# A two-layer perceiver in one launch: transposed inputs, regrouped first cross attention, and the second cross attention's normalisation and shift placed elsewhere

## What is computed

```python
x = x + _L0_xattn_ref(_layernorm(x), ctx, ctx, mask, Wq, bq, Wk, bk, Wv, bv, Wo, bo)  # 16 heads of 8
x = x + _L0_attn_ref(_layernorm(x), ...)      # delta rule over the tokens
x = x + _L0_ffn_ref(_layernorm(x), ...)       # 8 experts, the best 2
x = x + _L1_xattn_ref(ctx, _layernorm(x), Wq, Wkv, Wout, gm, bm, gl, bl)  # 8 heads of 64
x = x + _L1_attn_ref(_layernorm(x), ...)      # gated delta rule
x = x + _L1_ffn_ref(_layernorm(x), ...)       # attention, then 8 experts, the best 2
```

## Time and profile before

| | us |
|---|---|
| time, median of 3 (lowest, highest) | 3080.18 (3079.72, 3081.09) |
| profiled execution, its own time | 3079.37 |
| its span, first to last instruction | 3077.6 |
| mean granted TensorE clock | 0.962 |
| busy in the span: PE / DVE / ACT / POOL | 2819.4 / 1978.6 / 1479.6 / 1906.0 |

### The profile page before, as it was taken

How to read it: one execution, slowest core, us unless ns; L and a number is a source line. 1 busy time by engine, 2 the same in 40 slices (tenths; PEclk the granted TensorE clock), 3 DMA queues, 4 the chain that set the end, 5 groups by cost and what they waited for, 6 DMA issues and landing times. The chain is left out here.

```text
span 3077.6 us, 66754 instructions
## 1 busy us (share of the span) xinstructions
PE 2819.4 (92%) x22718; PEld 1618.6 (53%) x22765; DVE 1978.6 (64%) x4504; ACT 1479.6 (48%) x2385; POOL 1906.0 (62%) x1278
## 2 busy tenths in 40 slices
PE   5799999999999978998899999999999997888789
PEld 2355555555555566775344444444444443777356
DVE  5477777777777744114667767767767744776653
ACT  3466666666666522333544444444444434223633
POOL 5487878787878721001488888888888872553500
PEclk8899999999999989998999999999999998999789
DMA  7655555555555210001000000000000000000300
GB/s 184 187 174 193 177 190 181 184 186 179 194 175 188 100 58 1 1 0 39 22 33 21 21 32 21 21 32 21 21 32 21 21 1 9 3 3 2 85 5 10
DMA packets 146463, 233.18 MB, mean 76 GB/s; under 512 B 16787, under 2 KB 85851, under 8 KB 146076
## 3 DMA queue, kind: packets, MB, share of 16 engines
q1 hardware_dynamic: 145180, 228.87, 22.7%
q10 hardware_dynamic: 1152, 2.49, 0.6%
HBM read 147.80 MB, written 83.52 MB: 75 GB/s over the span
## 5 line engine op out<-in xcount | busy, mean ns | idle before, releaser
L444 POOL TENSOR_TENSOR sb_a_acc<-sb_a_acc,sb_a_PT 128x1024 f32<-128x1024 f32 x252 | 596.7, 2368 | 36.6 <-ACT sb_a_PT L522 30.3
L522 ACT ACTIVATE sb_a_PT<-ps_a_SC 128x1024 f32<-128x1024 f32 (+1 forms) x416 | 425.8, 1023 | 315.3 <-PE ps_a_SC L794 291.7
L607 DVE TENSOR_REDUCE sb_a_mx<-ps_a_A 128x1 f32<-128x512 f32 x768 | 506.4, 685 | 97.0 <-PE ps_a_A L771 91.8
L1686 POOL TENSOR_TENSOR sb_a_acc<-sb_a_acc,sb_a_PT 128x512 f32<-128x512 f32 (+2 forms) x384 | 487.5, 1269 | 37.3 <-ACT sb_a_PT L1782 10.9
L1782 ACT ACTIVATE sb_a_PT<-ps_a_SC 128x1024 f32<-128x1024 f32 (+2 forms) x256 | 234.3, 915 | 563.0 <-PE ps_a_SC L2061 329.3
L1875 DVE TENSOR_REDUCE sb_a_mx<-ps_a_A 128x1 f32<-128x512 f32 x384 | 256.5, 679 | 280.1 <-PE ps_a_A L2036 240.1
L2080 PE MATMUL ps_a_PV<-sb_a_PT,sb_a_XN 128*128 128x512 f32 (+2 forms) x896 | 434.3, 601 | 2.2 <-ACT sb_a_PT L1782 0.7
L2061 PE MATMUL ps_a_SC<-sb_a_QX,sb_a_XT 128*128 128x512 f32 (+1 forms) x832 | 396.7, 596 | 0.1
L771 PE MATMUL ps_a_A<-sb_a_KS,sb_a_QS 97*128 97x512 bf16 x768 | 301.9, 394 | 30.6 <-issue 17.7
L794 PE MATMUL ps_a_SC<-sb_a_QS,sb_a_KS 105*128 105x128 bf16 (+1 forms) x3328 | 257.3, 220 | 13.4 <-DVE sb_a_QS L621 13.4
L805 PE MATMUL ps_a_PV<-sb_a_PT,sb_a_V 128*32 128x256 f32 (+1 forms) x3328 | 266.7, 392 | 0.4 <-issue 0.3
(11 more groups left out here) (516 smaller groups left out, 5265.3 us busy)
## 6 DMA issues: line engine op xcount, KB each, us to landing
sb_a_C<-in_ctx_dram SPq DMA_DIRECT2D x64, 768.0 KB
a_KD<-sb_a_K SPq DMA_DIRECT2D x192, 256.0 KB, 4.1
sb_a_KS<-a_KD SPq DMA_DIRECT2D x256, 192.0 KB
a_KD<-sb_a_K SPq DMA_DIRECT2D x192, 144.2 KB, 2.7
sb_a_KS<-a_KD SPq DMA_DIRECT2D x256, 108.2 KB
sb_a_QP<-a_QD ACTq DMA_DIRECT2D x6, 384.0 KB, 14.7
sb_a_up<-in_moe_up_dram SPq DMA_DIRECT2D x1, 2048.0 KB, 7.9
sb_a_dn<-in_moe_dn_dram SPq DMA_DIRECT2D x1, 2048.0 KB, 12.0
```

What stands on the lines that cost most here:

```text
L444: pool.tensor_tensor(acc[:, :], first[:, :], PT[slot(a, j)][:, :], ALU.add).then_inc(s["acc"], 1)
L522: act.activation(PT[slot(a, j)][0:n, :], SC[(a + j) % 2][0:n, :], ACT.Exp).then_inc(s["exp"], 1)
L607: v.tensor_reduce(mx[:, p, c:c + 1], A[u % 2][:, :], AXX, ALU.max).then_inc(s["am"], 1)
L1686: pool.tensor_tensor(acc[a][0:m, :], first, PT[u % 4][0:m, HQ * i:HQ * i + HQ], ALU.add).then_inc(s["acc"], 1)
```

## The change

- The host passes the context transposed (`ctx_T`), and the weights transposed, repeated or side by side. The transposes, copies and some loads of weights go. The weights of the second cross attention are loaded in delta 0, those of feed-forward 1's attention in delta 1.
- All norms of x run in four chunks of four tiles, with the power of each chunk of its own; PE's transposes of chunks 2 and 3 stand later in some stages.
- First cross attention: PE, ACT and DVE work by groups of two tiles; chunks 0 and 1 of the keys are made a batch earlier; POOL sums tiles 0, 1, 2, 4, 5, 7, 8, 9 (`SUMS`), ones the other five; the scores of the next batch's first two tiles stand behind `total`; the maxima are transposed into A0; SP loads a context last in its step.
- Second cross attention: `shift` is left out; `c` = bm through the value and output weights of all heads is made once on PE, and POOL adds it to all of x; the latents' shift is `bl - bm`. The 13 normalisations go from DVE to ACT (`normed`, with -mean/std as the bias), chunk 0 at the end of the step before, chunks 1 to 3 at u = 1, 3, 5. DVE's `moments` go behind the last maximum.

The diff, cut to its core. The norm:

```diff
+    def moments(c):
+        tiles = range(4 * c, 4 * c + 4)
+        for n in tiles:
+            v.bn_stats(k.st6[:, n, :], src[:, n, :]).then_inc(s["stats"], 1)
+        for n in tiles:
+            v.wait_ge(s["stats"], n + 1)
+            v.bn_aggr(k.mv[:, n, :], k.st6[:, n, :]).then_inc(s["mean"], 1)
+        v.wait_ge(s["mean"], 5 * c + 4)
+        r, var = k.rstd[:, 4 * c:4 * c + 4], k.mv[:, 4 * c:4 * c + 4, 1]
+        if twice:
+            v.tensor_scalar(r, var, 1.0 + LN_EPS, LN_EPS * LN_EPS, ALU.mult, ALU.add).then_inc(s["mean"], 1)
+        else:
+            v.tensor_scalar(r, var, LN_EPS, None, ALU.add).then_inc(s["mean"], 1)
+
+    def scaled(c):
+        v.wait_ge(s["rstd"], c + 1)
+        for n in range(4 * c, 4 * c + 4):
+            v.tensor_scalar(dst[:, n, :], src[:, n, :], k.mv[:, n, 0:1], k.rstd[:, n:n + 1], ALU.subtract, ALU.mult)\
+             .then_inc(s["norm"], 1)
+
+    moments(0)
+    moments(1)
+    scaled(0)
+    moments(2)
+    scaled(1)
+    moments(3)
     if meanwhile is not None:
         meanwhile()
-    v.wait_ge(s["rstd"], 1)
-    for n in range(NT):
-        v.tensor_scalar(dst[:, n, :], src[:, n, :], k.mv[:, n, 0:1], k.rstd[:, n:n + 1], ALU.subtract, ALU.mult)\
-         .then_inc(s["norm"], 1)
+    scaled(2)
+    scaled(3)
```

```diff
-    COUNT = (0, 2, 2, 2, 2, 3, 3, 3, 3, 3, 3, 0, 0)
+    NG = (NK + 1) // 2
+    COUNT = (3, 5, 5, 5, 5, 3, 0)
+    SUMS = (1, 2, 4, 5, 7, 8, 9)
...
+                wait(sp, s["vp"], 4 * (b - 1))
+                sp.dma_start(CT[a][:, :], d["ctx_T"][dsl(b), :, :].rearrange("o d s -> d (o s)")).then_inc(s[f"ld{a}"], 16)
...
             def step(b, a, n2, n4):
-                if n4:
-                    load(b + 4, a)
                 if n2:
                     for g in range(2):
                         spill(b + 2, a, g)
-                    for g in range(2):
                         stack(b + 2, a, g)
+                if n4:
+                    load(b + 4, a)
```

ScalarE's step:

```diff
             def step(b, a, n1, n2, n3):
+                if n2:
+                    keys(b + 2, a, 2)
+                probs(b, a, 2)
+                probs(b, a, 3)
+                probs(b, a, 4)
+                if n2:
+                    second(b + 2, a, 2)
+                probs(b, a, 5)
+                if n2:
+                    keys(b + 2, a, 3)
+                probs(b, a, 6)
+                probs(b, a, 7)
+                if n2:
+                    values(b + 2, a, 0)
+                    second(b + 2, a, 3)
+                probs(b, a, 8)
+                probs(b, a, 9)
+                if n2:
+                    values(b + 2, a, 1)
+                probs(b, a, 10)
+                probs(b, a, 11)
+                if n3:
+                    keys(b + 3, 1 - a, 0)
+                probs(b, a, 12)
+                if n3:
+                    second(b + 3, 1 - a, 0)
+                    keys(b + 3, 1 - a, 1)
+                if n2:
+                    values(b + 2, a, 2)
+                if n3:
+                    second(b + 3, 1 - a, 1)
+                if n2:
+                    values(b + 2, a, 3)
+                if n1:
+                    for j in pair(0):
+                        probs(b + 1, 1 - a, j)
```

VectorE's step:

```diff
+            def step(b, a, n1, n2, n3):
                 old = not (isinstance(b, int) and b == 0)
                 if old:
                     emptied(b - 1)
+                if n2:
+                    residue(b + 2, 2)
+                for g in range(NG):
+                    for i, u in enumerate(units(g) if n1 else ()):
+                        tops(b + 1, u)
+                        if i == 3 and g == 1 and n2:
+                            residue(b + 2, 3)
+                        if i == 3 and g == 4 and n3:
+                            residue(b + 3, 0)
                 if n1:
                     top(b + 1)
+                if n3:
+                    residue(b + 3, 1)
+                if n1:
                     topped(b + 1, 1 - a)
                 if n2:
                     expand(b + 2, a)
+                if old:
+                    final(b - 1)
+                    invert(b - 1)
```

TensorE's keys and step:

```diff
+            def keys(b, a, c):
+
+                c0, n = ccols(c)
+                first = isinstance(b, int) and b < 2
                 if c == 0:
+                    pe.wait_ge(s[f"ld{a}"], 8 * (b - a) + 16)
+                    wait(pe, s["v"], 4 * b if isinstance(b, int) and b <= 2 else 4 * b - 2)
+                elif first:
+                    if c >= depth(b):
+                        wait(pe, s["kt"], 4 * b + c - depth(b) + 1)
+                else:
+                    wait(pe, s["kt"], 4 * b + c)
+                    if c == 2:
+                        wait(pe, s["v"], 4 * b)
                 pe.matmul(bank(b, 4 + c)[:, 0:n], k.w0T["k"], CT[a][:, c0:c0 + n], start=True, stop=True).then_inc(s["kp"], 1)
...
+                for g in range(NG):
+                    us = list(units(g)) if n1 else []
+
+                    def maxima(n):
+                        for u in us[0:n]:
+                            tops(b + 1, 1 - a, u)
+                        del us[0:n]
+
+                    if g == 0 and n2:
+                        keys(b + 2, a, 2)
+                    if g + 1 < NG:
+                        for j in pair(g + 1):
+                            if g > 0:
+                                maxima(1)
+                            scores(b, a, j)
+                        maxima(1)
+                    if g == 1 and n2:
+                        keys(b + 2, a, 3)
+                    if g == 2 and n2:
+                        values(b + 2, a, 0)
+                    if g in (4, 5) and n3:
+                        keys(b + 3, 1 - a, g - 4)
+                    if g > 0:
+                        maxima(1)
+                    if g == NG - 1 and n1:
                         top(b + 1)
+                    for j in pair(g):
+                        products(b, a, j)
+                    maxima(len(us))
+                    if g == 3 and n2:
+                        values(b + 2, a, 1)
+                    if g == 5 and n2:
+                        values(b + 2, a, 2)
                 total(b)
                 if n2:
                     values(b + 2, a, 3)
+                if n1:
+                    for j in pair(0):
+                        scores(b + 1, 1 - a, j)
```

```diff
-            def shift(b, a):
-
-                for lo, hi, m in ((0, KF, P), (KF, NK, SR)):
-                    pool.tensor_tensor(XN[a][0:m, lo:hi, :], XN[a][0:m, lo:hi, :], bmB[0:m, :].unsqueeze(1).to_broadcast([m, hi - lo, D]),
-                                       ALU.add).then_inc(s["xn"], 1)
...
+            pool.wait_ge(s["cbc"], 1)
+            pool.wait_ge(s["n"]["norm"], NT)
+            pool.tensor_tensor(k.x[:, :, :], k.x[:, :, :], cB[:, :].unsqueeze(1).to_broadcast([P, NT, D]), ALU.add).then_inc(s["cx"], 1)
...
+            def normed(b, a, c):
+
+                wait(act, s["nb"], b + 1)
+                for j in range(4 * c, min(4 * c + 4, NK)):
+                    m = wcols(j)
+                    act.activation(C[a][0:m, j, :], C[a][0:m, j, :], ACT.Identity, bias=nb[a][0:m, j:j + 1], scale=crs[a][0:m, j:j + 1])\
+                       .then_inc(s["z"], 1)
...
+                    if two and isinstance(b, int) and b == 0:
+                        if u == 4:
+                            for c in range(4):
+                                normed(2, 0, c)
+                    elif two and u in (1, 3, 5):
+                        normed(b + 2, a, (1, 3, 5).index(u) + 1)
...
+                    if three and u == 7:
+                        normed(b + 3, 1 - a, 0)
...
-                    if u == 4 and three:
-                        moments(b + 3, 1 - a)
...
-                    top(b + 1, 1 - a)
+                    top(b + 1)
                 if three:
-                    norm(b + 3, 1 - a)
-
-            v.wait_ge(s["ldw"], 16 * 10)
+                    moments(b + 3, 1 - a)
+                if one:
+                    topped(b + 1, 1 - a)
...
+            pe.wait_ge(s["bmm"], 1)
+            for h in range(H):
+                mm = pe.matmul(PV[:, 0:D], bmM[:, :], HH[:, h, :], start=(h == 0), stop=(h == H - 1))
+            mm.then_inc(s["cb"], 1)
```

More of the change, by code:

```diff
@@ L303, in dsl, with units, pair @@
         return bass.ds(b, 1)
-    def units(j):
-        return range(sum(COUNT[:j]), sum(COUNT[:j + 1]))
+    def units(g):
+        return range(sum(COUNT[:g]), sum(COUNT[:g + 1]))
+    def pair(g):
+        return tuple(j for j in (2 * g, 2 * g + 1) if j < NK)
     def summed(b):
-        return (1, 3, 5, 7, 9) if isinstance(b, int) and b == B - 1 else tuple(range(1, PTILE))
+        return (1, 3, 5, 7, 9) if isinstance(b, int) and b == B - 1 else SUMS
     def slot(a, j):
@@ L553, in _ @@
             for c in range(4):
-                turned(1, 1, c)
-            for c in range(4):
                 keys(1, 1, c)
@@ L561, in _ @@
                 values(1, 1, c)
-            for c in range(4):
```

(52 more changed lines are left out.)

376 lines of the change are left out of this document (139 added, 237 removed).

## The result

3171.4 us (median of 4 runs, 3168.1 to 3174.2) against 3080.4 us: 1.0295 times the kernel before, 95% interval 1.0277 to 1.0313. The change costs 91 us where 80 us less were forecast. The profiled execution has a span of 3170.4 us against 3077.6.

The account below looks back on a forecast made before the run. TensorE's instruction stream and its gaps were taken to bound both cross attentions, 1836 of 3078 us. Terms -63 - 2 - 8 + 21 - 27.5 = -79.5 against 3079.4 gave 3000 us, range 2950 to 3040.

Parts of the forecast that it names:

- SP's order: First cross attention: load(b+4) behind spill and stack delays nothing due before POOL's third, about 5 us into the next step.
- Rival (c): First cross attention: context load issued last, keys wait for landings beyond 16 us; slower from 18.8 us on; chance 0.04.
- -2.18: First cross attention: sum of all terms per step in us, giving a step of 29.1 us and -63 over 29 steps.
- waits of the earlier trace gone: First cross attention: TensorE waits of 0.73 us a step, with lead-in 0.98 us, taken as removable.
- new waits in brackets: First cross attention: scores 3 waits some 0.3 us, first units of group 1 about 0.5; in all +0.8 us a step.
- six visits: First cross attention: paired products need 7 visits to the 32-column matmuls instead of 13, 0.21 us each: -1.26 us a step.
- rival b: First cross attention gains little: VectorE paces middle groups or visits have no such price; step 30.3, total 3037 us; chance 0.25.
- -1.60: First cross attention: 13 context transposes removed from TensorE, -1.60 us a step.
- The ones' 0.86 us: First cross attention: tiles 3 and 6 summed by TensorE's ones instead of POOL, +0.86 us a step.
- The wait that was to appear for `normed` at the turn: Second cross attention: four normalisations on ScalarE delay the turn by 1.62 us in each of 29 steps: +46 us.
- The stall that was to go: Second cross attention: moments behind the maximum remove TensorE's wait, 1.67 us with lead-in every second step, 15 times: -25 us.
- Stage starts: Starts of delta 0 and 1, both feed-forwards and second cross attention: chunked norms and earlier weights, together -27.5 us.

Follow-up runs that it names:

- the experiment: The changed kernel, SyncE's order untouched, with the context load of batches 4 and later cut to 64 of 1601 columns: 3075.9 us.
- the kernel with the mended order: The changed kernel with both spills issued ahead of both stacks in SyncE's step of the first cross attention, as before the change: 3052.0 us, 0.9913 of the kernel before.
- the turn mended as well: The changed kernel with both spills ahead of both stacks, and the second cross attention's chunk 0 transposes and their copies one unit later: 3000.8 us, 0.9744.

## Why the prediction was wrong

**The step that failed** is one sentence in the part on the first stage: "SP's order: load(b+4) goes behind spill and stack ... Nothing else queued behind it is due". It followed the load past the queue and not the other item of the same diff, stack 0 moved ahead of spill 1. Each stack begins with a wait for the landing of its own spill, and I had followed only one of the two items that move. The sum to make was: 31.24 us a step less the 10.6 us that SyncE waited for others is 20.6 us of issuing; the changed queue has two landings in a row, for which the trace of before has this row (L353, 300 to 900):

```profile
DMA to landing us min/median/max: 1.8/3.4/5.1
```

With the longest of them 20.6 + 2 x 5.1 = 30.8 us. That is above the 29.1 us forecast, before any landing gets longer behind the load: nearly all of the stage's gain would have been gone. It is still below 31.24, so the loss of 91 us needed two things that the rows of before do not show: stands of 6.0 us each (210.7 / 35), and 22.0 us of issues in a step. Together they make 34.0 us, and the step listed above has 33.97.

**Rival (c)** was the nearest: slower, by the context load behind the stacks. It named a wrong victim, the keys' own wait for the load. There is no such wait: the load lands in 7.2 us (median), far below its 16. The rival had 0.04. The load does lengthen the landing behind it, 95 us by the experiment, in a loop that the rival didn't see.

**The step without the loop**: -1.4 us measured (29.8 us between two steps of the kernel with the mended order, against 31.24) where -2.18 was forecast. The parts: waits of the earlier trace rows gone, as said; new waits in brackets 0.51 + 0.29 = 0.80 us, as said to the hundredth, which is luck in a term that I took as a round sum; six visits at 0.22 us, -1.3 as forecast; and three hidden stands of 0.28 us at VectorE's pace, +0.84, which I had bounded (rival b) and not summed. With the forecast's other terms this adds up: -1.60 + 0.86 - 1.3 - 0.98 + 0.80 + 0.84 = -1.4. Of the 0.98 only 0.73 are waits that a row shows. The ones' 0.86 us is a true cost of TensorE, but no choice: without it GpSimd is late.

**The second cross attention** went as worked out. The wait that was to appear for `normed` at the turn was forecast at 1.62 us a step and is 44.9 / 27 = 1.66; four normalisations take 1.64 us against 1.62. The rows of ScalarE won over the estimate from the figure of the Trainium skill (VectorE: DVE Perf Modes, The TRN2 errata), by which they would have taken 1.2 us. The stall that was to go, 1.67 in every second step, gave 66.2 - 64.7 = 1.5, and the new wait costs 68.2 - 64.7 = 3.5 in two steps instead of 3.24. So a pair of steps is 2.0 us longer; 14.5 of them make +30 where +21 was forecast, and the stage's +19.0 leaves -11 for its start, of -10 forecast.

**Stage starts**: -27.5 forecast; -10 in the second cross attention as said, 0 in delta 0 with feed-forward 0 (of -5.5), -6.3 in the last two stages (of -12). Feed-forward 1's up projections start 10.9 us earlier against the stage before, 4.6 of it are gone at the end. The term took an earlier start for a gain at the stage's end. In feed-forward 0 half of it went to the low clock, at which the first long matmuls now run, and half to the transposes and the copy that the change put behind them; for the other stages this was not worked out. The start of the first stage gave 2.7 us (137.9 to 135.2) of the 8.

With SyncE's order mended the time would have been 3052, above the range still; with the turn mended as well, 3000.8. That this is the forecast number is chance: the forecast had the turn's wait in it.

## What to carry to other kernels

For each queue that issues transfers, add up a step: issue times, plus every wait for a landing that has nothing between itself and the transfer that it waits for. Compare the sum with the new step that you forecast, not with the old one; slack of such a queue is its waits for others. Two transfers that depend on each other through memory want other work of the queue between them. And mean slack of an engine is no room: see in which place of its queue the result stands that others wait for.

## What the hardware showed beyond that

In the changed kernel the granted clock of TensorE falls after a stand of 2.34 us in the first stage: it is 1.00 from 617 to 620 us, TensorE then stands until 621.40, and from 624 to 627 it is 0.55, for the most part the lower of its two levels (1.2 of 2.4 GHz).

```profile
617.00:620.00 3.00, 2.07 (x26) 0.92 (x25) 0.00 (x0) 0.81 (x2) 2.99 (x2) 1.00 0.19 59
624.00:627.00 3.00, 3.00 (x27) 1.14 (x26) 1.67 (x3) 1.71 (x4) 2.78 (x2) 0.55 0.52 141
```

This comes in 22 of the 31 steps and makes the stage's 0.94. With stands of at most 0.6 us (mended order) the clock stays at 1.00 throughout. In the closed loop the slow stretch itself costs little, I think, since SyncE sets the pace there; no run separates that.

What stands ahead of a transfer in the queue shows in its landing: the 256 KB transfers of spill 0 land at 3.4 us in the median behind a load of 32 KB, at 6.3 behind one of 800 KB, and at 7.7 where the load and the sixteen transfers of both stacks go ahead of them (mended order). The 144 KB transfers of spill 1 land at 4.9 and 4.7 us behind stack 0 with the small and the large load, so in these two runs the size of the load reaches only the transfers right behind it.
